# Causal attention on one Trainium2 core: softmax sums by GpSimd additions and one product, causal mask added by VectorE

## What is computed

```
x = x + attn_a(layernorm(x))   # squared scores instead of a softmax
x = x + ffn(layernorm(x))      # gated: softmax attention, keys and values picked by a gate
x = x + attn_b(layernorm(x))   # one key head and one value head for all queries
x = x + ffn(layernorm(x))
```

```
# attn_a: q and k normalized per head
attn = where(mask, einsum('bqhd,bkhd->bhqk', q, k) ** 2, 0.0)
o = einsum('bhqk,bkhd->bqhd', attn, v) / (sum(attn, -1) + EPS)
# ffn and attn_b
scores = where(causal, einsum('bhqd,bkd->bhqk', q, k) * scale, -inf)
y = einsum('bhqk,bkd->bhqd', softmax(scores), v)
```

## Time and profile before

| | |
|---|---|
| median of 3 runs | 4797.77 us (4794.02 to 4806.56) |
| the profiled execution | 4810.55 us, span 4808.8 us |
| busy: PE, DVE, ACT, POOL | 4292.6, 1770.6, 1546.9, 847.3 us |
| mean granted TensorE clock | 0.961 of full speed |
| DMA traffic | 115.67 MB, mean 24 GB/s |

### The profile page before, as it was taken

How to read it: one execution, slowest core, us unless ns; L and a number is a source line. 1 busy time by engine, 2 the same in 40 slices (tenths; PEclk the granted TensorE clock), 3 DMA queues, 4 the chain that set the end, 5 groups by cost and what they waited for, 6 DMA issues and landing times.

```text
span 4808.8 us, 76616 instructions
## 1 busy us (share of the span) xinstructions
PE 4292.6 (89%) x32674; PEld 1781.0 (37%) x32674; DVE 1770.6 (37%) x2666; ACT 1546.9 (32%) x1985; POOL 847.3 (18%) x1495
## 2 busy tenths in 40 slices
PE   6899999996999898898898989989899897988987
PEld 4343434333333333333333333333333333333333
DVE  1222212122544444434444443443443444444342
ACT  1433333340223323323333333332222233232333
POOL 1311212121101211202112221211112012011012
PEclk8999999998999999999999999999999999999999
DMA  1001010003000100101001010000001001010010
GB/s 62 18 1 36 18 36 18 18 18 102 18 1 1 54 1 23 32 1 38 16 23 32 12 43 1 25 30 26 28 1 46 9 1 54 1 37 17 1 36 27
DMA packets 63405, 115.67 MB, mean 24 GB/s; under 512 B 8672, under 2 KB 9184, under 8 KB 63072
## 3 DMA queue, kind: packets, MB, share of 16 engines
q1 hardware_dynamic: 63072, 110.77, 7.2%
HBM read 77.19 MB, written 33.55 MB: 23 GB/s over the span
## 4 chain that ended last, share of the span: by engine, by line
PE 58%; DVE 6%; issue 5%; ACT 3%; DMA 2%; POOL 2%; POOLq 0%; SPq 0%; DVEq 0%; ACTq 0%
PE banks L1085 14%; PE banks L1043 10%; PE banks L995 9%; PE banks L1027 8%; PE banks L988 7%; DVE maxima_soft L811 5%; PE banks L1024 3%; ACT probs_soft L732 3%; PE banks L1052 2%; PE banks L1184 2%; DMA tiles_soft<-out 1%; PE banks L1159 1%; PE banks L1094 1%; POOL tiles_soft L637 0%; POOL rest_soft L705 0%
## 5 line engine op out<-in xcount | busy, mean ns | idle before, releaser
L811 DVE TENSOR_REDUCE maxima_soft<-banks 128x2 f32<-128x1024 f32 (+3 forms) x1152 | 1036.6, 953 | 1309.8 <-PE banks L1052 828.6
L732 ACT ACTIVATE probs_soft<-banks 128x1024 f32<-128x1024 f32 (+1 forms) x960 | 848.5, 936 | 1252.4 <-PE banks L1027 1250.2
L1043 PE MATMUL banks<-k_soft,q_soft 32*128 32x512 f32 (+3 forms) x4608 | 547.0, 544 | 69.6 <-ACT probs_soft L732 67.6
L646 POOL TENSOR_SCALAR_AFFINE_SELECT probs_soft<-probs_soft 128x512 f32<-128x512 f32 x384 | 239.2, 635 | 1963.5 <-ACT probs_soft L732 1961.8
L1027 PE MATMUL banks<-q_soft,k_soft 32*128 32x512 f32 (+3 forms) x4608 | 487.1, 505 | 0.0
L1085 PE MATMUL banks<-probs_soft,v_soft 128*32 128x512 f32 (+3 forms) x4608 | 435.6, 497 | 13.4 <-ACT shift_soft L718 9.5
L1085 PE MATMUL banks<-probs_soft,ones 128*32 128x512 f32 (+3 forms) x4608 | 433.5, 495 | 0.0
L732 ACT ACTIVATE probs_squared<-banks 128x1024 f32<-128x1024 f32 (+1 forms) x320 | 282.8, 936 | 387.7 <-PE banks L1027 387.6
L1043 PEld LDWEIGHTS banks<-k_soft,q_soft 32*128 32x128 f32 x4608 | 187.1, 186 | 320.1 <-issue 302.3
L1024 PE MATMUL banks<-shift_soft,ones 32*128 32x512 bf16 (+3 forms) x2304 | 202.3, 339 | 113.9 <-DVE maxima_soft L811 100.9
L995 PE MATMUL banks<-g_wv,xnT_soft 128*128 128x512 f32 x512 | 251.4, 625 | 27.4 <-DVE inverse_soft L917 21.2
(11 more groups left out here) (151 smaller groups left out, 4218.7 us busy)
## 6 DMA issues: line engine op xcount, KB each, us to landing
tiles_soft<-out SPq DMA_DIRECT2D x96, 256.0 KB, 2.9
rest_soft<-out SPq DMA_DIRECT2D x96, 256.0 KB, 3.0
out<-rest_soft SPq DMA_DIRECT2D x96, 256.0 KB, 2.0
tiles_squared<-in_x SPq DMA_DIRECT2D x32, 256.0 KB, 2.9
rest_squared<-in_x SPq DMA_DIRECT2D x32, 256.0 KB, 2.9
out<-rest_squared SPq DMA_DIRECT2D x32, 256.0 KB, 2.0
raw_wq<-in_squared_wq SPq DMA_DIRECT2D x1, 1024.0 KB, 6.2
raw_wk<-in_squared_wk SPq DMA_DIRECT2D x1, 1024.0 KB, 8.5
```

Source lines behind the costliest of these rows:

```text
L646: ins = pool.affine_select(out=cells, in_=cells, compare_op=ALU.is_ge, fill=0.0, base=0, pattern=[[0, HG], [1, P]], channel_multiplier=-1)
L732: act.activation(slot(ph, n)[:, 2 * a:2 * a + 2, 0:width], score_pair(e, a)[:, :, 0:width], ACT.Exp if soft else ACT.Square, scale=SCALE). ...
L811: ins = dve.reduce_max(m["maxima"][:, ph % 2, 2 * a:2 * a + 2, t, p], score_pair(e, a)[:, :, col:col + P * blocks], AX_X)
L1043: ins = pe.matmul(psum[:, score_bank(e, i), col:col + P * blocks], m["q"][D * i:D * i + D, ph % NG, P * t:P * t + P], k_of(ph)[D * i:D * i ...
```

## The change

Sums: GpSimd adds up the masked probabilities of all key blocks of a chunk into a new tensor `added` (event `add`, eight per phase: one with a copy ahead of it, some in two pieces), three half-steps after the burst; one product with ones per chunk (`sm`, now a unit per chunk, not per part) follows. A slot is now free after its value product and its addition, and there are 5 slots. ScalarE takes the sums of both chunks out of PSUM; VectorE's addition for part C's sums goes.

Maxima: on diagonal blocks the mask products go. VectorE adds a mask of up to 512 columns and takes the maximum in one `tensor_tensor_reduce` for each head; the sum is written back over the scores in PSUM.

Squared phases: the key's scale goes into the square, one activation for each head and key block with a scale by partition, where one took two heads. It is the power -1/2 of the variance, made by GpSimd (L734 of the changed kernel). The values are no longer scaled.

```diff
-SLOTS = 6
+SLOTS = 5
...
+ADDS = {1: [(384, 128, 384)], 2: [(0, 256, 256)], 4: [], 5: [(0, 512, 0)], 6: [(0, 512, 0)], 7: [(0, 512, 0)],
+        8: [(0, 384, 128), (384, 128, 384)], 9: [(0, 256, 256)]}
...
+SUMS_AT = (12, 6)
...
+    for n in ADDS:
+        if n < NKB - 1:
+            at[2 * n + 3].append(("add", ph, n))
+    if ph:
+        at[1].append(("add", ph - 1, NKB - 1))
...
+                elif u == "add":
+                    _, ph, n = e
+                    c, part, parts = KEY_BURSTS[n]
+                    pool.wait_ge(sg.probs_ready, 2 * (of_kind["keys", ph, n] + 1))
+                    pool.wait_ge(sg.probs_masked, masks_until(ph, part, n))
+                    total = m["added"][:, c]
+                    if n in (1, 4):
+                        if ph:
+                            wait_work(pool, ("sm", ph - 1, c))
+                        if n == 1:
+                            pool.tensor_copy(total[:, :, 0:P], slot(ph, 0)[:, :, 0:P])
+                            ins = pool.tensor_tensor(total[:, :, P:CHUNK], slot(ph, 0)[:, :, P:CHUNK], slot(ph, 1)[:, :, 0:CHUNK - P], ALU.add)
+                        else:
+                            ins = pool.tensor_tensor(total, slot(ph, 3), slot(ph, 4), ALU.add)
+                    else:
+                        pool.wait_ge(sg.probs_added, len(ADDS) * ph + ADD_AFTER[n] - 1)
+                    for x, (col, width, q0) in enumerate(ADDS[n]):
+                        if x or n == 1:
+                            then(ins)
+                        sums = total[:, :, q0:q0 + width]
+                        ins = pool.tensor_tensor(sums, sums, slot(ph, n)[:, :, col:col + width], ALU.add)
+                    ins.then_inc(sg.probs_added, 1)
...
+                            for kb, _, cols, col in parts:
+                                for x in range(2):
+                                    i = 2 * a + x
+                                    ins = act.activation(slot(ph, n)[:, i, col:col + cols], score_pair(e, a)[:, x, col:col + cols],
+                                                         ACT.Square, scale=m["key_scale"][:, ph % NG, kb, i:i + 1])
...
-                            ins = dve.reduce_max(m["maxima"][:, ph % 2, 2 * a:2 * a + 2, t, p],
-                                                 score_pair(e, a)[:, :, col:col + P * blocks], AX_X)
+                            width = P * blocks
+                            if p < t // TPC:
+                                ins = dve.reduce_max(m["maxima"][:, ph % 2, 2 * a:2 * a + 2, t, p],
+                                                     score_pair(e, a)[:, :, col:col + width], AX_X)
+                                continue
+                            for x in range(2):
+                                scores = score_pair(e, a)[:, x, col:col + width]
+                                ins = dve.tensor_tensor_reduce(scores, scores, k["mask"][:, CHUNK - width:CHUNK], 1.0, MASKED, ALU.add,
+                                                               ALU.max, m["maxima"][:, ph % 2, 2 * a + x, t, p:p + 1])
...
+                elif u == "sm":
+                    _, ph, c = e
+                    out = free(e)
+                    if not soft:
+                        pe.wait_ge(sg.query_squares, place["qsq", ph, c] + 1)
+                        pe.matmul(out, k["head_eps"][:].rearrange("p i d -> p (i d)"), m["query_square"][:, c], start=True, stop=True)
+                    pe.wait_ge(sg.probs_added, len(ADDS) * ph + CHUNK_ADDS[c])
+                    for i in range(HG):
+                        ins = pe.matmul(out[D * i:D * i + D, :], k["ones"][:], m["added"][:, c, i, :], start=soft, stop=True,
+                                        skip_group_check=not soft)
+                    ready(e, ins)
```

141 lines of the change are left out of this document (65 added, 76 removed).

## The result

The changed kernel takes 4742.39 us (median of 4 runs, 4741.89 to 4749.11), the kernel before, run beside it, 4798.87: a ratio of 0.9886, 95% interval 0.9873 to 0.9898. The change gains 56 us, 1.2%, where 200 were forecast.

A forecast was written before the change was run, and what follows sets the result against it. TensorE, busy 89%, bounds the kernel, but bare waits limit the gain: gated stages 120, mqa 94, squared 70, sum 284 us, less 8 (row bursts), 15 (ends) and 60 (clock), leaving 200: 4600 us, range 4480 to 4720.

The forecast's parts named there:

- The bare phase: Second phase of a gated stage, only bursts, value products and sums: 56 us against 54.7, 1 lost.
- the fourth: Fourth phase of a gated stage, value projections fill the waits: 69.0 us comes to about 60, 9 gained.
- hidden in sum, not in order: GpSimd in a bare phase: its 7.4 us become 40 of some 54.
- some 2.8 us of TensorE waiting in bare phases, under 1 where there is filler: Soft phases: K9's mask, queued behind a 4.5 us GpSimd addition, is ready at 60.2 us, the value product at 57.4.
- eat what this phase saves: First phase of a gated stage: 5 to 8 us of new waits at the stage change, so 0 gained.
- The squared phases: 16 phases, 6.5 us saved each at most; with stage changes and GpSimd's 45 us, 17.5 a stage, 70 in all.
- The third gated phases and the mqa ones: Third phase of a gated stage: 7.5 us gained; mqa (product) stages: 23.5 each, 94 in four.
- The clock: TensorE's granted clock falls by 0.07 in sparse phases: 3.8 us on 54, 60 in some sixteen phases' worth.
- rival (d): TensorE's clock falls further, sparse phases at 0.80: about 4770 us, chance 0.13; sign: under 0.9 without stage change.
- Rival (c): VectorE's masked sweep costs its upper bound, 1.37 us, 7 us more per bare phase: 4800 to 4850 us, chance 0.10.
- (b): GpSimd's additions cost far more than 4.5 us and it becomes the bound: 4990 us at 9 us each, chance 0.05.
- (a): TensorE stays the bound, its waits filled elsewhere: 4220 to 4480 us, say 4320, chance 0.20.

The follow-up runs named there:

- short additions: The changed kernel with every GpSimd addition and the copy cut to 16 columns per head, same instructions, order and waits, output wrong: 4544.40 us.
- The fill: The changed kernel with four dummy 128x512 products on TensorE ahead of each burst that follows a burst with no other work between: 4688.69 us.

## Why the prediction was wrong, step by step

**What held.** The prices: 4.52 against 4.49 us for an addition, 0.86 against 0.83 for a sweep with its write-out. The bare phase (+1.4 for +1) and the fourth (-9.0 for -9): taking work out of bare waits gives nothing, as read from the earlier trace rows. TensorE's waits at the end: from the last phase's first exponential on it is 76.7 us, 16 more than before. The squares are hidden but for some 7 us. Together, all that is not the length of GpSimd's additions came out at 254 us of gain (short additions against the kernel before, 4798.87 less 4544.40), 54 more than the whole forecast.

**The step that failed** is the pricing of GpSimd's queue: "hidden in sum, not in order", then "some 2.8 us of TensorE waiting in bare phases, under 1 where there is filler", and in a gated first phase waits that "eat what this phase saves". Measured, the occupation by additions costs 198 us: 60 in the squared stages, 95 in the gated ones, 41 in the mqa ones. Of these the forecast had the 17 us of the last phase (it took 15 for both ends) and, with 2.8 us, the 2.2 of a second phase. What it set aside at the stage changes did not even go to the additions' length: the first gated phases gain nothing with short additions either (80.0 us against 79.5), where by the timelines above the new order is at work, and the squared stages then gain 58 of the 104 us that TensorE saves there. The queue came on top, in three places:

- The first phase of a gated stage. The forecast had the right chain (output sum, store, load, statistics, transposes) and both places too: the last output directly ahead of the first transpose, and an addition between the tiles. It put 5 to 8 us there and held that what the phase saves pays them. The first place alone took that much (3.25 us became 10.13, with short additions 10.09); the second, 7.30 us, came on top. The phase lost 6.7 us in the mean of the table (3.0 with the gated stage that it leaves out) and 12.5 in the stage shown, and short additions give 6.2 and 7.0 of it back.
- The squared phases. The forecast had "hidden" for ScalarE's squares, and for GpSimd only that its 45 us exceed the barest phase; it priced waits neither for key squares (11.3 us became 52.2, 27.5 with short additions) nor for masks (2.1 became 33.7, then 8.1). They gained nothing instead of 70.
- The third gated phases and the mqa ones. 3.7 us a third phase and 10 us an mqa stage stand against "under 1".

The cover was argued by load (40 of 54 us). But GpSimd, busy for 42 to 68% of the four phases shown, works through its queue in order with pieces of 4.5 us, and a small step behind one of them is late; here normalised tiles, key squares, masks, scaled outputs and the maxima's steps all feed TensorE.

**The clock.** The forecast took 60 us off for 0.90 instead of 0.97 and gave a clock under 0.9 in phases without a stage change as the sign of rival (d). That sign came: 0.83 in a bare phase. The fill, which takes it to 1.00 there and the mean halfway back, returned 54 us net of its own products. So the clock costs at least about what the forecast took off, and possibly some of (d)'s further 110 us; the runs don't say how much. The reason is one that the forecast did not give: at 1.2 GHz the score products between two waits take 1.94 instead of 1.04 us. That (d)'s 4770 us is the nearest of the four to the measured time is in good part luck, since it has no cost for GpSimd's queue, and shorter additions alone give 198 us. The same clock may be why TensorE was busy for 3850 us and not for the 3700 forecast. Rival (c) is out by the sweep's price, (b) by the addition's, (a) by the bare waits.

What stays open: the short additions shorten both the queue's other steps and the way from the last addition to the product with ones. TensorE's waits put down to the latter are small (5.5 us), but the two were not tried apart. They also free VectorE, which the long additions hold up (last section): its busy time falls by 52 us. Of TensorE's waits only the 10 us for picking can be put down to that directly; what it does through other engines was not tried. Nor was it tried what the old order between the last output and the new tiles would give back, why the squared stages fall 46 us short of their 104 with short additions, or whether the fifth instead of the sixth slot costs anything.

## What to carry to other kernels

Work that is moved to an idle engine is not paid by its load but by what queues behind it: list every small step of that engine on which the bottleneck waits, and charge each of them up to one of the new long instructions, then cut these or give part of them back (a third of the additions returned to TensorE gained 49 us). A wait for an engine need not come from its load: compare it with the new instructions shortened, and see what stood between two dependent steps before and stands there no more (3.25 us became 10.13 so, and stayed 10.09). Try the halves of a change separately: here one gave 87 us and the other took 30 of them back. Where a change leaves the product engine with gaps, look at the granted clock of the stretch; a few dummy products in bare gaps gained 54 us at a mean clock of 0.918, but only 11, not clear of the scatter, at 0.959.

## What the runs showed of the hardware

A VectorE operation can stand still for a whole GpSimd addition. L961 multiplies two tensors in SBUF; its 32 instances (shortest, median, longest in ns) and one of them beside GpSimd's timeline:

```profile
L961 DVE TENSOR_TENSOR y_squared<-y_squared,sums_squared x32: 691/693/4733, 151.4 to 1099.1; 128x512 f32<-128x512 f32 x32
```

```profile
204.78 4.66 DVE L961 TENSOR_TENSOR y_squared<-y_squared,sums_squared 128x512 f32<-128x512 f32 x1
204.38 4.51 POOL L681 TENSOR_TENSOR added_squared<-probs_squared 128x2048 f32<-128x2048 f32 x1
```

The median is unchanged, but the longest took 4.73 us. The one at 204.78 started 0.4 us into an addition and ended (at 209.44) only after it (at 208.89). In the kernel with short additions the longest is 835 ns, before it was 694. The Trainium skill (GPSIMD Engine Reference, Specifications) says that GpSimd and VectorE contend where VectorE has two SBUF inputs or is in a 2-port performance mode; the trace agrees, and shows the size, up to the length of the GpSimd instruction. Three small steps that choose the gate are held as well: L901 and L904, with two SBUF inputs, take up to 3296 and 3427 ns where the longest before were 293 and 294, and L902, with one, up to 3340 where it was 228. The forecast weighed this for the masked sweep alone, whose other input is in PSUM (723 ns beside long additions and beside short ones), and missed these four.

A power with 16 columns costs GpSimd 2912 ns where one with a single column costs 551 (L654): 157 ns a column, far from the 2.1 ns an element of an addition.
